# First key and query weights by quarters, first norms in another order, passes over ones ahead of the first weights, measured lengths in the plan

## The reference

```
# per batch element: x is 2048 x 1024, 16 heads of 64
h = layernorm(x)
Q, K, V = h @ Wq + bq, h @ Wk + bk, h @ Wv + bv
scores = Q K^T / 8 + mask          # mask[i, j] = -inf for j > i, else -0.25 * log(i - j)
x = x + softmax(scores) V @ Wo + bo
h = layernorm(x)                   # then a complex-valued linear layer, W unfolded from small factors
x = x + [hr Wr' - hi Wi', hr Wi' + hi Wr'] + bias
```

## Time and profile before

| | |
|---|---|
| time before, 3 runs | median 563.18 us (561.47 to 565.92) |
| time of the profiled execution | 561.32 us |
| its span (core 7, the slowest) | 559.8 us; the other cores 555.4 to 558.1 us |
| PE busy | 517.1 us (92%) |
| DVE, ACT busy | 461.3 us (82%), 381.9 us (68%) |
| granted clock, core 7 | 0.996; the others 0.999 or 1.000 |

### The profile page before, as it was taken

One profiled execution on the slowest core, in us unless ns is written; L12 is line 12 of the kernel. 1 busy time (PEld: TensorE's weight loads), 2 busy tenths in 40 slices (PEclk: granted clock), 3 DMA queues, 4 the chain that ended last, 5 costly groups with the idle time before them and its releaser, 6 DMA issues.

```text
span 559.8 us, 16753 instructions; the slowest of 8 cores (555.4 to 559.8 us)
## 1 busy us (share of the span) xinstructions
PE 517.1 (92%) x6096; PEld 241.2 (43%) x6096; DVE 461.3 (82%) x830; ACT 381.9 (68%) x526; POOL 38.3 (7%) x51
## 2 busy tenths in 40 slices
PE   1798989899999999989999999999999999999986
PEld 1334444344443444444444444444545444444442
DVE  5645999999999999887777887887888888888683
ACT  3425776778888879866767777777778777786010
POOL 7000000000000000000000020201101011111110
PEclk9999999999999999989999999999999999999999
DMA  8999231000120000010000089756566666457574
GB/s 200 187 170 253 78 114 39 3 2 2 40 78 2 8 34 1 2 47 33 1 3 2 1 121 185 150 137 148 135 152 152 152 151 141 97 130 171 146 153 150
DMA packets 16479, 52.77 MB, mean 94 GB/s; under 512 B 2000, under 2 KB 2000, under 8 KB 15632
## 3 DMA queue, kind: packets, MB, share of 16 engines
q0 software_dynamic: 7328, 28.05, 27.5%
q1 hardware_dynamic: 9072, 23.65, 12.7%
HBM read 51.69 MB, written 8.39 MB: 107 GB/s over the span
## 4 chain that ended last, share of the span: by engine, by line
PE 69%; DVE 9%; ACT 8%; issue 7%; DMA 5%; DVEq 0%; ACTq 0%; POOLq 0%
PE gp L1057 18%; PE stP L1118 11%; PE pv L1142 10%; PE gp L1093 8%; PE gp L1067 8%; PE gp L1103 8%; ACT PT L996 5%; PE pr L1148 4%; DMA Wo<-wo 3%; PE gp L1044 2%; DMA x<-bfn 1%; DVE stat L700 1%; DVE x L773 1%; DVE V L748 1%; DVE attnT L874 1%
## 5 line engine op out<-in xcount | busy, mean ns | idle before, releaser
L996 ACT ACTIVATE PT<-stP,negc 128x1024 bf16<-128x1024 f32 (+1 forms) x320 | 301.4, 983 | 81.8 <-PE stP L1120 80.1
L857 DVE TENSOR_TENSOR PT<-PT,decay 128x1024 bf16<-128x1024 bf16 (+1 forms) x320 | 190.7, 603 | 35.0 <-ACT PT L996 33.2
L1142 PE MATMUL pv<-PT,V 128*32 128x256 bf16 (+3 forms) x2560 | 101.4, 258 | 1.5 <-DVE PT L857 0.5
L1118 PE MATMUL stP<-QT,KT 64*128 64x512 bf16 (+1 forms) x320 | 94.5, 350 | 5.2 <-ACT PT L996 5.0
L1120 PE MATMUL stP<-QT,KT 64*128 64x512 bf16 (+1 forms) x320 | 95.1, 352 | 0.0
L1148 PE MATMUL pr<-PT,ones 128*32 128x256 bf16 (+3 forms) x1280 | 81.2, 257 | 0.7 <-issue 0.7
L1067 PE MATMUL gp<-Wv,xnT 128*128 128x512 bf16 x256 | 67.3, 385 | 8.6 <-DVE V L748 5.0
L1142 PEld LDWEIGHTS pv<-PT,V 128*32 128x32 bf16 x2560 | 56.7, 96 | 38.2 <-issue 35.9
L1057 PE MATMUL gp<-xnT,Wk 128*128 128x512 bf16 x256 | 66.7, 389 | 2.5 <-ACT xnT L968 2.0
L1057 PE MATMUL gp<-xnT,Wq 128*128 128x512 bf16 x256 | 65.0, 380 | 1.0 <-DVE KT L755 0.9
L1093 PE MATMUL gp<-Wo,attnT 128*128 128x512 bf16 x256 | 63.3, 380 | 2.4 <-DVE x L773 1.7
(11 more groups left out here) (71 smaller groups left out, 432.1 us busy)
## 6 DMA issues: line engine op xcount, KB each, us to landing
xrot<-x SPq DMA_DIRECT2D x21, 512.0 KB, 4.5
x<-bfn POOLq DMA_DIRECT2D x16, 512.0 KB, 6.4
out<-outb SPq DMA_DIRECT2D x32, 256.0 KB, 3.3
xrot<-bo POOLq DMA_DIRECT2D x12, 512.0 KB, 5.8
xfirst<-x SPq DMA_DIRECT2D x4, 512.0 KB, 6.2
Wk<-wk POOLq DMA_DIRECT2D x2, 1024.0 KB, 21.3
Wq<-wq POOLq DMA_DIRECT2D x2, 1024.0 KB, 27.0
Wv<-wv POOLq DMA_DIRECT2D x2, 1024.0 KB, 32.6
```

The source lines that it names most:

```text
L857: v.tensor_mul(pt, pt, decay[:, off + no:off + 512].unsqueeze(1).to_broadcast([128, 2, 512 - no])).then_inc(s_pm, 1)
L996: a.activation(p_tile(g, no), st_tile(g, no), AF.Exp, bias=negc[:, c * 8 + p % 2 * 4 + p // 2:][:, 0:1]).then_inc(s_exp, 1)
L1118: t.matmul(stP[g % 2][:, no:512], KT[0:64, ks:ks + 128], QT[0:64, qs + no:qs + 512], start=True, stop=True, tile_position=(0, 0))
L1142: t.matmul(pv[x:x + 32, half * 256 + no // 2:(half + 1) * 256], V[:, vo + h * 64 + half * 32:vo + h * 64 + half * 32 + 32], p_part(g, h, a ...
```

## The change

Four things are changed.

1. The layout of Wq and Wk in memory goes from two halves to four quarters of 256 columns. The first half of each is loaded as two DMAs with a semaphore each, the second half as one. K(0, 0) waits for the first quarter alone, K(0, 2) for the second, and likewise for Q.
2. In the plan, A of tile 2 comes after S2 of tile 3, and M 0 and QB come after the eviction of T(3) (before: after A of tile 3).
3. PE runs matmuls of 512 columns over a column of ones, into `stP[0]`: 22 ahead of everything, 7 ahead of T(1), 4 ahead of T(2), 3 ahead of K(0, 0). Nobody reads their result; scores overwrite it.
4. The lengths of the plan are set anew: nearly all ACT and DVE tasks are shorter, and the constant from an end to its users goes from 0.12 to 0.18. `make_fill` is not touched.

```
+LAG = 0.18
+WARM = {0: 22, ("T", 1): 7, ("T", 2): 4, ("K", 0, 0): 3}
...
-                us = {"B": 0.3, "T": 0.65}.get(what, 0.67)
+                us = {"B": 0.25, "K": 0.67, "Q": 0.67}.get(what, 0.61)
...
-        task("act", ("X", g), 0.19 + 0.00088 * w, ("S", g), g and ("X", g - 1), g >= PR and ("V", g - PR),
+        task("act", ("X", g), 0.14 + 0.000853 * w, ("S", g), g and ("X", g - 1), g >= PR and ("V", g - PR),
...
-        task("dve", ("P", g), 0.03 + 0.00063 * w, ("X", g), ("P", g - 1) if g else ("M", 3))
+        task("dve", ("P", g), 0.068 + 0.00052 * w, ("X", g), ("P", g - 1) if g else ("M", 3))
...
-        task("dve", ("Z", n), 1.35, ("Y", n), n in (24, 28) and ("D", ("N", 3, 2 + (n - 24) // 4)),
+        task("dve", ("Z", n), 1.22, ("Y", n), n in (24, 28) and ("D", ("N", 3, 2 + (n - 24) // 4)),
...
-        task("dve", ("A", n), 0.75, ("R", n), n and ("A", n - 1), n >= 2 and ("D", ("T", n - 2)))
+        task("dve", ("A", n), 0.72, ("R", n), n and ("A", n - 1), n >= 2 and ("D", ("T", n - 2)),
+             n == 2 and ("S2", 3))
...
-    task("dve", ("M", 0), 2.8, ("A", 3))
+    task("dve", ("M", 0), 2.8, ("E", ("T", 3)))
...
-    for name, us in (("wka", 19.0), ("wqa", 26.0), ("wva", 34.0), ("wkb", 40.0), ("wqb", 47.0), ("wvb", 54.0), ("g", 62.0)):
+    for name, us in (("wka0", 16.0), ("wka1", 19.0), ("wqa0", 22.5), ("wqa1", 25.5), ("wva", 34.0), ("wkb", 40.0), ("wqb", 47.0), ("wvb", 54.0), ("g", 62.0)):
...
-            return tasks[k][1] + (0.4 if engine == "act" and k[0] == "E" and k[1][0] == "T" else 0.0)
+            more = {"T": 0.31, "K": -0.08, "Q": -0.08}.get(k[1][0], 0.0) if engine == "act" and k[0] == "E" else 0.0
+            return tasks[k][1] + more
...
-                finish(k, end + 0.12)
+                finish(k, end + LAG)
...
+            def quarter(dst, src, q, got):
+                g.dma_start(out=dst[:, q * 2048:(q + 1) * 2048], in_=src[q]).then_inc(got, 16)
+
+            def last_quarters(dst, src, got):
+                g.dma_start(out=dst[:, 4096:8192].rearrange("p (q n) -> p q n", q=2),
+                            in_=src[2:4].rearrange("q p n -> p q n")).then_inc(got, 16)
...
-            weight(Wk, dwk, 0, s_w["wk_a"])
-            weight(Wq, dwq, 0, s_w["wq_a"])
+            quarter(Wk, dwk, 0, s_w["wk_a0"])
+            quarter(Wk, dwk, 1, s_w["wk_a1"])
+            quarter(Wq, dwq, 0, s_w["wq_a0"])
+            quarter(Wq, dwq, 1, s_w["wq_a1"])
             load_bv(0)
             weight(Wv, dwv, 0, s_w["wv_a"])
-            weight(Wk, dwk, 1, s_w["wk_b"])
-            weight(Wq, dwq, 1, s_w["wq_b"])
+            last_quarters(Wk, dwk, s_w["wk_b"])
+            last_quarters(Wq, dwq, s_w["wq_b"])
...
-                        piece = {0: "_a", 4: "_b"}.get(p)
+                        piece = {0: "_a0", 2: "_a1", 4: "_b"}.get(p)
...
-                        o = p // 4 * 4096 + k * 512 + p % 4 * 128
+                        o = p // 2 * 2048 + k * 256 + p % 2 * 128
...
+            def warm(passes):
+
+                for _ in range(passes):
+                    t.matmul(stP[0][:, 0:512], ones32[:, 0:1].to_broadcast([128, 128]),
+                             ones32[:, 0:1].to_broadcast([128, 512]), start=True, stop=True)
+
+            t.wait_ge(s_const, 4)
+            warm(WARM[0])
             for what, *n in PE_ORDER:
+                if what == "G" and n[0] in WARM and n[1] == 0:
+                    warm(WARM[n[0]])
```

More of the change, by code:

```diff
@@ L252, in make_orders @@
                   "B": [("BM",) + lab[1:]], "O": [("Z", n // 4 * PAIRS + PAIRS - 1)], "F": [("E", ("T", NT + n)), n == 0 and ("WR", 7)]}[what]
-            of += [("dma", "w" + what.lower() + "ab"[(lab[2] // 4 if what in "KQ" else lab[2])])] if (
+            of += [("dma", "w" + what.lower() + ({0: "a0", 1: "a1"}.get(lab[2] // 2, "b") if what in "KQ" else "ab"[lab[2]]))] if (
                 what in "KQ" and n == 0) or (what == "V" and n < 4) else []
-            us = {"T": 0.12 if what == "T" and n < 4 else 0.06, "N": 0.08, "B": 0.3}.get(what, 0.216) * (k1 - k0)
+            us = {"T": 0.06, "N": 0.08, "B": 0.3}.get(what, 0.216) * (k1 - k0)
             task("pe", k, us, *((of + [bank(groups.index(lab))]) if k0 == 0 else []))
@@ L288, in make_orders @@
         x = [("dma", "x", n)] * 2 if n < NT else [("E", ("O", n - NT, h)) for h in range(2)]
[L289 to L292 removed]
+        task("dve", ("S1", n), 0.6, x[0], n and ("S2", n - 1), n >= 4 and ("A", n - 4))
+        task("dve", ("S2", n), 0.83, x[1], ("S1", n))
+        task("act", ("R", n), 0.53, ("S2", n), n and ("R", n - 1))
+        task("dve", ("A", n), 0.72, ("R", n), n and ("A", n - 1), n >= 2 and ("D", ("T", n - 2)),
+             n == 2 and ("S2", 3))
         if n < NT:
@@ L300, in make_orders @@
         n = c * 4 + p // 2 - 2
-        task("dve", ("SQ", c, p), 0.75, ("E", ("K", c, p)), ("E", ("Q", c, p)), i and ("SQ",) + pairs[i - 1],
+        task("dve", ("SQ", c, p), 0.67, ("E", ("K", c, p)), ("E", ("Q", c, p)), i and ("SQ",) + pairs[i - 1],
              n >= 0 and ("D", ("N", n // 4, n % 4)))
@@ L305, in make_orders @@
             before = (c, 0) if h else (c - 1, 1) if c else None
[L306 to L309, removed]
-    task("dve", ("M", 0), 2.8, ("A", 3))
+            task("dve", ("BD", c, h), 0.13, ("E", ("N", c, 2 * h)), ("E", ("N", c, 2 * h + 1)), before and ("BL",) + before)
+            task("act", ("BL", c, h), 0.19, ("BD", c, h), c and ("D", ("B", c - 1, h)))
+            task("dve", ("BM", c, h), 0.08, ("BL", c, h), before and ("BM",) + before, c and ("D", ("B", c - 1, h)))
+            task("dve", ("BN", c, h), 0.08, ("E", ("B", c, h)), before and ("BN",) + before)
+    task("dve", ("M", 0), 2.8, ("E", ("T", 3)))
     task("act", ("M", 1), 2.4, ("M", 0))
@@ L337, in latest @@
                 else:
-                    late[k] = min([pe_at.get(u, late.get(u)) for u in users[k]] + [1e4]) - tasks[k][1] - 0.12
+                    late[k] = min([pe_at.get(u, late.get(u)) for u in users[k]] + [1e4]) - tasks[k][1] - LAG
                     stack.pop()
@@ L438, in build_program @@
     dx = nc.dram_tensor("x", [SEQ, D], F32, kind="ExternalInput").ap()
-    dwq = nc.dram_tensor("wq", [2, 128, FT * 512], F32, kind="ExternalInput").ap()
-    dwk = nc.dram_tensor("wk", [2, 128, FT * 512], F32, kind="ExternalInput").ap()
+    dwq = nc.dram_tensor("wq", [4, 128, FT * 256], F32, kind="ExternalInput").ap()
+    dwk = nc.dram_tensor("wk", [4, 128, FT * 256], F32, kind="ExternalInput").ap()
     dwv = nc.dram_tensor("wv", [2, 128, FT * 512], F32, kind="ExternalInput").ap()
@@ L463, in build_program @@
         s_fb = [sem(f"x2_plus_bf{j}") for j in range(4)]
-        s_w = {n: sem(n) for n in ("wk_a", "wk_b", "wq_a", "wq_b", "wv_a", "wv_b", "wo_in")}
+        s_w = {n: sem(n) for n in ("wk_a0", "wk_a1", "wk_b", "wq_a0", "wq_a1", "wq_b", "wv_a", "wv_b", "wo_in")}
         s_ident, s_cols, s_g = sem("ident_in"), sem("cols_in"), sem("g_in")
@@ L1214, with columns @@
             cols[64 * par + 32 + h, 16 + h * 2 + par] = 1
-    wq, wk, wv = (np.ascontiguousarray(w.reshape(FT, 128, 2, 512).transpose(2, 1, 0, 3).reshape(2, 128, FT * 512))
-                  for w in (wq, wk, wv))
+    def columns(w, n):
+        return np.ascontiguousarray(w.reshape(FT, 128, n, D // n).transpose(2, 1, 0, 3).reshape(n, 128, D // n * FT))
+    wq, wk, wv = columns(wq, 4), columns(wk, 4), columns(wv, 2)
     wo = np.ascontiguousarray(wo.reshape(4, 2, 2, 2, 32, D).transpose(0, 3, 1, 2, 4, 5).reshape(D, D))
```

6 lines of the change are left out of this document (3 added, 3 removed).

## The result

The changed kernel takes 568.58 us (median of 20 runs each) against 564.27 us for the kernel before in the same 20 rounds. The ratio is 1.0079, with a 95% interval of 1.0051 to 1.0107. I had forecast 559.0 in a range of 553.5 to 564.0. The measured time is outside, and on the other side of the kernel before.

What follows compares the result with a forecast made beforehand. Bound by the start before the first projection, mostly through PE, plus PE idle of 8.4 and 8.1 us later. 563.2 less 3.1 (start) and 1.0 (new order) gave 559.1, stated as 559.0; range 553.5 to 564.

Steps and rivals of the forecast that it cites:

- Part 4: Order of all three engines, made anew from truer lengths: taken as -1 us, bounded by -6 us and rival C.
- rival C: At O(0, 0): fewer PE steps before it leave PE waiting for Wo; 569 from 40 passes moved; chance 0.06.
- rival A: Steady part or end: new order takes 4 to 6 us of idle time besides the start's gain; 555.0; chance 0.31.
- Sum of the start: Everything up to the first projections: 3.7 us on core 7, 2.9 on core 0; 3.1 taken for the slowest core.
- part 1: First norms: reordering lets K(0, 0) start at 17.25, at worst 17.9; gain 1.9 us, at least 1.2.
- The cut by Wv: At V(0, 0) on core 0: Wv's unmoved landing cuts the start's gain from 4.3 to 2.9 us.
- What is won stays: From start to end: a loss at the start isn't won back, so the 3.1 us won should stay.
- Part 3: Passes over ones ahead of K: K passes run at the upper clock; gain 1.8 us (1.3 to 2.4).
- the fall that I called chance: Core 7, 240 to 260 us: granted clock 0.91, about 1.8 us, chance that the change doesn't touch.
- Part 2: Weight loads: quarters of Wk and Wq land in time, no wait; Wv 1.3 us later if cover is gone.

Runs made afterwards that it cites:

- e2: The kernel before with the new lengths and the new constant in the plan alone; ratio 1.0165.
- e3: The change with the lengths and the constant of before, the order made anew from them; ratio 0.9953.
- e5: The change with the lengths of DVE's tasks and of the evictions as before; ratio 0.9970.
- e6: The change with ACT's lengths and the constant as before, DVE's lengths new; ratio 1.0036.
- e9: The change with the length of P (multiplication by the decay) alone put back to the old; ratio 0.9972.
- e16: The kernel before with the new length of P alone; ratio 1.0042.
- e14: The change with P's length at 0.72 us for full width, longer than the old; ratio 1.0004.
- e7: e3 with Wo loaded as two DMAs by column halves, order untouched; ratio 0.9875 on three executions, 557.84 us.
- e8: The change with Wo loaded in two column halves, order untouched; ratio 1.0011.
- e1: The kernel before with quarters, passes over ones and the first norms' order written by hand, the rest of the order old; ratio 0.9982.
- e10: e7 without the passes over ones; ratio 0.9926.
- e11: e7 with the first half of Wk and of Wq loaded as one DMA each; ratio 0.9939, 558.38 us.

## Why the prediction was wrong, point by point

**Part 4, the lengths, is the step that failed.** I argued that the new lengths are truer, because one eviction of V is followed by the next instruction 0.61 us later, and gave the new order a gain of 1 us within -6 and rival C. It cost: e2 has nothing else in it and stands at 1.0165, and e3, without it, stands at 0.9953 where the change stands at 1.0079. So the term that I put at -1 us measured about +7 us. Most of the single lengths are truer indeed. In the full stretch of the kernel before, P at full width is followed by the next DVE instruction after 0.60 us in the median, V's eviction after 0.61. But the sum isn't. The DVE tasks of core 1 from P of step 25 to P of step 91 add up to 101.3 us by the old lengths and to 94.4 us by the new ones, and they took 99.5. Of the 5.1 us that are missing, 2.0 are one length: Z, two instructions, takes 1.42 us from its start to the next start, as in these two rows of core 1, and the new length is 1.22 (the old one 1.35).

```profile
100.81 1.39 DVE L874 TENSOR_TENSOR attnT<-pv,recip 64x512 bf16<-64x512 f32 x2
102.23 0.69 DVE L748 TENSOR_TENSOR V<-gp,bvB 128x512 bf16<-128x512 f32 x1
```

Idle time of DVE, in which an instruction waits for the one it depends on, is 1.9 us (0.3 of it behind Z), and the rest is small parts of many tasks. The old lengths had all of it inside by being too long elsewhere (P at full width 0.675 for 0.60). With 5 us of every 100 missing, the plan sees free slots on DVE that don't exist, and fills them with steps of W and evictions of K and Q, seven more by 200 us. P comes later for it, and V of the steps behind P, on PE. That DVE's lengths are the cause is shown (e5 against e6; of P's length alone e9 and e16). That they act by the tasks put ahead of P is read from the orders and agrees with all plans but e14; it was not tried by itself, and neither was Z's length alone.
I had the row that spoke against me, DVE at 136.4 of 140 us, and explained it away in rival A: that 0.69 is counted for each 0.61. The right use of it was to add up the plan's lengths over that stretch. I also read the chain as going nearly wholly through PE. The page of the kernel before gives PE 69% of it, and DVE and ACT 17% together:

```profile
PE 69%; DVE 9%; ACT 8%; issue 7%; DMA 5%; DVEq 0%; ACTq 0%; POOLq 0%
```

**Rival C was named, but its condition was wrong, and that its 569 was nearly met is luck.** I made it depend on the new order putting fewer steps between K(3, 7) and O(0, 0), and priced it with a standstill of 8.7 us. The order didn't: without a wait O(0, 0) starts 18.1 us after the last K in the kernel before, in the change and in e3. The standstill was 4.7 us at most, and core 1, which has none, is 4.9 us slower than before. What varies is the load: 16.3 to 18.6 us on the eight cores before, 22.3 and 21.4 us on cores 0 and 5 after, and 21.8 us on core 3 of e3. A margin of nothing was there all along. e7 and e8 take the load off: from 1.0079 to 1.0011 is 3.8 us for the change, and from 0.9953 to 0.9875 is 4.4 us for e3. Why a load is slow is open. Cores 0 and 5 of the change were 2.9 and 2.7 us behind cores 1 and 4 at their last K, against 0.4 and 1.3 us in the other two pairs; but core 7 of e6 was only 0.7 us behind core 6 and had a load of 21.4 us and a wait of 3.9.

**Sum of the start: its size 0.8 us too high, and part 1 is the term that was too large.** I took 3.1 us. In the change the first exponent came 0.9 to 3.7 us earlier than on the same core before, 2.3 in the mean of the eight. Part 1 was to bring K 1.9 us earlier, at least 1.2, to 17.25, at worst 17.9. K started at 17.7 to 18.8 us in the change, 1.1 us earlier in the mean, and at 17.5 to 18.7 in e7, 1.3 us earlier. The transpositions take 0.61 us in the timeline instead of 1.01, as I wanted, but A of tile 2 began at 14.26 on core 1 and not at 13.9. Where the order of evictions goes with it (e7), the 32 passes take 6.9 us (as said), and the first exponent is 3.1 to 4.2 us earlier on cores 0, 2, 4 and 6 than before, 0.7 to 0.9 on 5 and 7, and 1.2 to 1.4 later on 1 and 3, where Wv lands at 35.1 and 34.9 us and the clock falls in the wait (granted 0.997 on both). The cut by Wv came, but on other cores than I thought: before, the even cores were the late ones. "What is won stays" holds as long as the order is the same and no later load is met: step 0 to 128 is 207.6 us in the kernel before on seven cores and in e1 on four. On three cores of e1 tile 6 of x took 1.3 to 2.0 us of it back, and in e7 core 6 lost 1.8 us in the same way. I had used it across two orders, where it says nothing, and I had looked for the cut at Wv alone.

**Part 3, the passes.** In the profiled execution of the change the clock fell at 17 us on four of eight cores. I had let gaps of 1.7 us or less pass, and written that the rows before had none over 1.0 us. They had: core 7 idled 1.16 us at 108 us and 1.19 us at 242.6 us, and the fall that I called chance came 2 us behind the second. Core 1 has a gap of 1.18 us at the same place and no fall, so the gap alone doesn't decide. In the change the order put A of tile 1 ahead of S2 of tile 2, so T(2) came at 16.04 on core 0, where in e7 it came at 14.63, and PE idled 1.86 us ahead of it, with 3.57 of 7 us busy. The Trainium skill says ("TensorE: Matmul & The Clock Gate", HAM oscillation) that idle gaps re-throttle the engine, and the trace agrees in part: the clock fell behind the gap on four cores (granted clock 0.57 from 17 to 21 us on core 0), and on the other four the same gap did nothing. In e7, where T(2) comes earlier, no core fell there, and the passes are worth 2.1 to 2.9 us (e10).

**Part 2.** No wait of K or Q for a quarter, as said. The rule that small DMAs are dear ("DMA: Bandwidth & Descriptors", Bandwidth, in the Trainium skill) would have put Wv 1.2 us later; the means of e7 and e11 (33.0 and 33.1 us) don't show it.

## What to carry to other kernels

A list scheduler's lengths have to be right in their sum over the stretch in which an engine is full: add them up over such a stretch and set the sum beside the time that it took, before and after a recalibration, task by task, from start to next start. A length that was too long may have paid for another that is too short. A load that the plan doesn't know, and that lands just in time in one profile, is a wait in the next execution; cut it so that the first user needs half of it. When the start gets quicker, the evictions behind it must be planned with it, and every load behind it looked at, not the next one alone, or they take the gain.

## What the runs showed of the hardware

A short fall of the granted clock costs about 1.5 us (209.1 us from step 0 to 128 on core 7 of the kernel before, 207.6 on the seven others; 212.5 against 210.9 in e16). Between these steps the change has one or two such falls on each core, the kernel before one in all eight. On core 1 of the change it came at 246 us, in a 20 us window with PE busy 17.56 us, behind gaps of 0.88 and 0.85 us, none of them longer. Core 1 of the kernel before has 17.62 us of busy time there, a gap of 1.18 us, and no fall. The same idle time is followed by a fall on one core and not on another, so whether a given gap costs a fall can't be told from these rows.

Matmuls over a single column of ones bring the clock up: 22 of them, from 1.47 us on, took 6.2 to 7.8 us on the eight cores of the change; they start 0.43 us apart at first and 0.22 us apart at the end.
